# Memory projections of a fused two-layer network: the dot products of keys move from VectorE and GpSimd to TensorE

## The reference, cut to what matters

```python
k = k / jnp.maximum(jnp.linalg.norm(k, axis=-1, keepdims=True), 1e-12)
alpha = jax.nn.sigmoid(alpha_raw) * 0.5
...
def t_step(M, kv):
    k_t, v_t = kv
    Mk = jnp.einsum('bhde,bhe->bhd', M, k_t)
    forget = Mk[..., :, None] * k_t[..., None, :]
    write = v_t[..., :, None] * k_t[..., None, :]
    return (M - alpha * forget + beta * write, None)
```

## Time and profile before

| | |
|---|---|
| timed runs | 4588.27, 4594.0, 4600.99 us; median 4594.0 |
| profiled execution | 4591.41 us, span 4589.7 us, mean granted clock of PE 0.891 |
| busy over the span | PE 3650.9, DVE 2555.3, POOL 1683.4, ACT 1439.0 us |
| the stage `mproj` | from 2539.8 us (its first DMA issue) to 2970.5 us (the first of the next stage) |

### The profile page before, as it was taken

How to read it: one execution, slowest core, us unless ns; L and a number is a source line. 1 busy time by engine, 2 the same in 40 slices (tenths; PEclk the granted TensorE clock), 3 DMA queues, 4 the chain that set the end, 5 groups by cost and what they waited for, 6 DMA issues and landing times. The chain is left out here.

```text
span 4589.7 us, 53885 instructions
## 1 busy us (share of the span) xinstructions
PE 3650.9 (80%) x17474; PEld 1655.7 (36%) x17563; DVE 2555.3 (56%) x3976; ACT 1439.0 (31%) x2018; POOL 1683.4 (37%) x1362
## 2 busy tenths in 40 slices
PE   8899999979997899977695404077897956999994
PEld 3322222223332433325353202033455433555553
DVE  5589999945552255534425597855794693111113
ACT  2247777743332233322132202011452311111111
POOL 0032222226664066652362273533561332222221
PEclk9979999989998999988797756588897978999997
DMA  5542322211103511013326202033452103333333
GB/s 174 185 72 63 68 71 61 56 55 37 37 24 100 180 35 37 26 61 99 101 86 197 102 18 73 18 87 91 134 163 97 46 19 107 103 94 95 98 86 82
DMA packets 323883, 382.97 MB, mean 83 GB/s; under 512 B 52016, under 2 KB 252992, under 8 KB 322688
## 3 DMA queue, kind: packets, MB, share of 16 engines
q1 hardware_dynamic: 270912, 285.83, 20.2%
q0 software_dynamic: 35776, 73.97, 6.4%
q10 hardware_dynamic: 17024, 20.97, 1.3%
HBM read 240.69 MB, written 135.76 MB: 82 GB/s over the span
## 5 line engine op out<-in xcount | busy, mean ns | idle before, releaser
L571 DVE TENSOR_REDUCE modulated_mx<-modulated_ring 128x1 f32<-128x512 f32 x1024 | 651.5, 682 | 51.7 <-PE modulated_ring L478 45.7
L555 ACT ACTIVATE modulated_probs<-modulated_scores 128x1024 f32<-128x1024 f32 x512 | 496.1, 1021 | 181.5 <-PE modulated_scores L499 181.4
L2862 DVE TENSOR_TENSOR expert_h<-expert_gelu,expert_bank 128x512 f32<-128x512 f32 x128 | 88.0, 688 | 391.8 <-PE expert_bank L2830 391.8
L2790 POOL DMA_INDIRECT scratch_acc<-expert_y,expert_idx x64 | 101.0, 1579 | 485.2 <-DVE expert_y L2867 443.2
L508 PE MATMUL modulated_acc<-modulated_probs,modulated_v 128*32 128x512 f32 x2048 | 273.6, 606 | 0.6 <-ACT modulated_probs L555 0.6
L478 PE MATMUL modulated_ring<-modulated_k,modulated_q 64*128 64x512 bf16 x1024 | 239.6, 399 | 34.1 <-DMA modulated_v<-scratch_v 23.0
L499 PE MATMUL modulated_scores<-modulated_q,modulated_k 128*128 128x512 bf16 x945 | 255.6, 383 | 10.1 <-issue 5.4
L910 POOL TENSOR_TENSOR causal_total<-causal_total,causal_probs 128x1024 f32<-128x1024 f32 x96 | 225.7, 2351 | 86.5 <-ACT causal_probs L831 85.5
L910 POOL TENSOR_TENSOR meta_total<-meta_total,meta_probs 128x1024 f32<-128x1024 f32 x96 | 225.7, 2351 | 86.5 <-ACT meta_probs L831 85.5
L2830 PE MATMUL expert_bank<-expert_xT,expert_wg 128*128 128x512 f32 x512 | 243.2, 598 | 7.8 <-ACT expert_xT L2842 7.8
L853 DVE TENSOR_REDUCE meta_mx<-meta_maxima 128x2 f32<-128x1024 f32 x120 | 146.0, 1216 | 184.0 <-PE meta_maxima L737 184.0
(11 more groups left out here) (471 smaller groups left out, 7028.7 us busy)
## 6 DMA issues: line engine op xcount, KB each, us to landing
expert_wg<-x_WgT SPq DMA_DIRECT2D x16, 1024.0 KB, 4.9
expert_wu<-x_WuT SPq DMA_DIRECT2D x16, 1024.0 KB, 6.9
expert_wd<-x_WdT SPq DMA_DIRECT2D x16, 1024.0 KB, 5.4
modulated_k<-scratch_k_part SPq DMA_DIRECT2D x192, 64.0 KB, 3.0
modulated_q<-scratch_q_part SPq DMA_DIRECT2D x192, 64.0 KB, 3.1
scratch_v<-proj_v SPq DMA_DIRECT2D x8, 1024.0 KB, 6.6
modulated_v<-scratch_v SPq DMA_DIRECT2D x16, 512.0 KB, 4.5
scratch_M<-steps_snap SPq DMA_DIRECT2D x16, 512.0 KB, 3.3
```

The costliest lines, as they stand in the source:

```text
L555: nc.scalar.activation(probs[u % NPROBS][i][:], sc[i][:], ACT.Exp, scale=SCALE).then_inc(s_exp, 1)
L571: V.tensor_reduce(mx[h % 2][:, x // 2, 1 - j % 2, j // 2, x % 2:x % 2 + 1], ring[bank_of["max", 4 * m + j]][:], AX.X, ALU.max).then_inc(s_ ...
L2790: added[j].done(G.indirect_dma_start(out=scr["acc"], out_offset=bass.IndirectOffsetOnAxis(ap=idx[j][a][:], axis=0), in_=y[j][:, a, :], in_ ...
```

## The change: what it does

- **Dot products on PE.** POOL makes from the transposed keys `laid` two masked copies per tile of 128 tokens (`masked`, L1820): one keeps the even heads, one the odd heads, both multiplied by -alpha (`share_of`). PE multiplies them with `laid` (L1856 of the changed file), 16 matmuls of 128 columns per tile, each on a row group of 32 rows, which is one pair of heads; neighbouring matmuls take different row groups p and write different banks. This gives for every head the 128 x 128 dot products of the tile's tokens, with -alpha in them.
- **Eviction.** ACT (in group 0 ACT and DVE, two banks each; in group 1 ACT all four) copies the banks to `dots`, two buffers.
- **Transfers lay them by piece.** Of each 128 x 128 square only the eight 16 x 16 blocks on the diagonal are wanted. SP issues 8 DMAs per tile (L1793), one per piece: 16 partitions x 16 heads x 16 tokens into one partition of `A`, which is 256 runs of 64 bytes, 16 KB. With 16 tiles that is 128 DMAs per group, 256 in all. The products, sums, the clearing and the scaling of `A` on DVE and POOL go.
- **DVE alone substitutes,** both halves of the heads in whole, in place in `k` (the copy S goes).
- **Groups overlap.** There is no hardware loop: the code is written out (class `Order` numbers the steps), `xT`, `k`, `A` have two buffers, both `xT` loads are issued at the start, by SP. While DVE substitutes group 0 it also makes the keys of group 1 (after each of its first five steps), and PE, POOL, ACT and SP make group 1's dot products. The projections of v and q of both groups come last on PE and ACT, beside the substitution of group 1.

The diff, cut to its core:

```diff
-            with sp.Fori(0, N // GROUP) as g:
-...
-                dve_s.wait(dve, g, ("k", TT - 1, QUADS - 1))
-...
-                    pool_s.wait(dve, g, ("far", n))
-                    dve_s.done(total(other[n % 2], f[1], f[0]), ("far", n))
-...
+        jobs = []
+        for g in range(G):
+            for c in range(QUADS):
+                jobs += [("k", g, c)] + [("kT", g, c - 1, m) for m in range(HH)] * (c > 0)
+            jobs += [("kT", g, QUADS - 1, m) for m in range(HH)]
+            jobs += [("dots", g, t) for t in range(TILES)]
+        for g in range(G):
+            for c in range(QUADS):
+                jobs += [("v", g, c)] + [("q", g, c, m) for m in range(KD)]
+...
+        ACT_BANKS = {0: (0, 1), 1: (0, 1, 2, 3)}
+        STEPS = range(SUB - 1, 0, -1)
+...
+            for g in range(G):
+                act_s.wait(sp, ("kT", g, QUADS - 1, HH - 1))
+                sp.dma_start(rows(scr["kT"])[:, :, g * GROUP:(g + 1) * GROUP], laid[:]).then_inc(s_kT, 16)
+                for t in range(TILES):
+                    act_s.wait(sp, ("dots", g, t, ACT_BANKS[g][-1]))
+                    if g == 0:
+                        dve_s.wait(sp, ("dots", g, t, 3))
+                    for s in range(PIECES):
+                        r = slice(s * SUB, (s + 1) * SUB)
+                        n = t * PIECES + s
+                        sp.dma_start(A[g][n:n + 1, :, :, :], dots[t % 2][r, :, r]).then_inc(s_laid[t % 2], 16)
+            dve_s.wait(sp, ("rows", 0, 1, 1))
+            sp.dma_start(by_piece(scr["s4"][0:GROUP, :]), k[0][:]).then_inc(s_s, 16)
+...
+            for g in range(G):
+                act_s.wait(pool, ("kT", g, QUADS - 1, HH - 1))
+                for t in range(TILES):
+                    if t >= 2:
+                        mm.wait(pool, ("dots", g, t - 2))
+                    here = laid[:, :, t * P:(t + 1) * P].unsqueeze(2).broadcast_to([P, HH, 2, P])
+                    pool_s.done(nc.gpsimd.tensor_tensor(masked[t % 2][:], here, share_of[:].unsqueeze(3).broadcast_to([P, HH, 2, P]), ALU.mult),
+                                ("masked", g, t))
+...
+                if kind == "dots":
+                    pool_s.wait(pe, ("masked", g, c))
+                    for half in range(HH):
+                        for odd in range(2):
+                            for p in range(4):
+                                r = slice(p * PAIR, (p + 1) * PAIR)
+                                last = nc.tensor.matmul(at[p][:, (2 * half + odd) * P:(2 * half + odd + 1) * P], masked[c % 2][r, half, odd, :],
+                                                        laid[r, half, c * P:(c + 1) * P], start=True, stop=True)
+...
+                for t in range(TILES):
+                    mm.wait(act, ("dots", g, t))
+                    use = g * (TILES // 2) + t // 2
+                    if use > 0:
+                        act.wait_ge(s_laid[t % 2], 16 * PIECES * use)
+                    for p in ACT_BANKS[g]:
+                        from_ = bank[banks_of(("dots", g, t))[p]]
+                        act_s.done(copy(dots[t % 2][:].rearrange("p (a b o) n -> p a b o n", a=HH, o=2)[:, :, p, :, :], from_[:].rearrange("p (a o n) -> p a o n", a=HH, o=2)),
+                                   ("dots", g, t, p))
+...
+                    for part in range(HALVES):
+                        if i + 1 < SUB:
+                            dve_s.wait(dve, ("rows", g, i + 1, part))
+                        elif g > 0:
+                            dve_s.wait(dve, ("rows", g - 1, 1, part))
+                        dve_s.done(tt(laid_out(part), A[g][:, i, part * HP:(part + 1) * HP, 0:i].rearrange("p h r -> p r h").unsqueeze(3).broadcast_to([P, i, HP, HD16]),
+                                      k[g][:, i:i + 1, heads(part)].rearrange("p r (h e) -> p r h e", e=HD16).broadcast_to([P, i, HP, HD16]), ALU.mult),
+                                   ("share", g, i, part))
+                    for part in range(HALVES):
+                        dve_s.wait(dve, ("share", g, i, part))
+                        dve_s.done(tt(k[g][:, 0:i, heads(part)], k[g][:, 0:i, heads(part)], own[part][:, 0:i * HP * HD16].rearrange("p (r n) -> p r n", r=i), ALU.add),
+                                   ("rows", g, i, part))
+                    if g == 0 and n <= QUADS:
+                        if n > 0:
+                            make_keys(1, n - 1)
+                        if n < QUADS:
+                            measure(1, n)
```

More of the change, by code:

```diff
@@ L1652, in every_16th, with __init__, done, wait @@
     return a.rearrange("p (s x) -> p x s", x=SUB)
+class Order:
+    def __init__(self, sem, names, passed):
+        self.sem, self.passed, self.at = sem, passed, 0
+        self.value = {x: n + 1 for n, x in enumerate(names)}
+        assert len(self.value) == len(names)
+    def done(self, ins, name):
+        self.at += 1
+        assert self.value[name] == self.at, (name, self.at)
+        return ins.then_inc(self.sem, 1)
+    def wait(self, eng, name, alone=False):
+        eng.wait_ge(self.sem, self.value[name])
+        if alone:
+            apart(eng, self.passed)
@@ L1672, in memory_projections @@
         length2, length, bounded, inv = (st.sb(n, [P, TT * H16]) for n in ("length2", "length", "bounded", "inv"))
[L1673 to L1676 removed]
         laid = st.sb("laid", [P, HH, GROUP])
+        masked = two("masked", [P, HH, 2, P])
+        dots = two("dots", [P, H16, P])
@@ L1700, in memory_projections @@
-        for n, (f, e) in enumerate(zip(far, near)):
-            dve_names += [("near", n)] * (e is not None) + [("far", n)] + [("near_sum", n)] * (e is not None)
-        dve_names += [("scaled", hp) for hp in range(HH)]
-        for i in range(SUB - 1, 0, -1):
-            dve_names += [(x, i, part) for x in ("share", "rows") for part in range(2)]
-        act_s, dve_s = st.steps("act", act_names), st.steps("dve", dve_names)
-        pool_s = st.steps("pool", [("far", n) for n in range(len(far))] + [(x, i) for i in range(SUB - 1, 0, -1) for x in ("share", "rows")])
@@ L1708, in memory_projections @@
-        PARTS = ((0, 0, HP), (1, 0, HP // 2), (1, HP // 2, HP))
-        loaded = st.moves("loaded", credit=0, kept=True)
-        stored = {x: st.moves("stored_" + x, HH if x in ("v", "s") else 1) for x in ("q", "v", "kT", "s")}
-        s_w, s_made, s_alpha = st.sem("weights"), st.sem("made"), st.sem("alpha")
+            dve_names += lengths(0, c) + keys(0, c)
+        dve_names += [("dots", 0, t, p) for t in range(TILES) for p in range(4) if p not in ACT_BANKS[0]]
+        for g in range(G):
+            for n, i in enumerate(STEPS):
+                dve_names += [(x, g, i, part) for x in ("share", "rows") for part in range(HALVES)]
+                if g == 0 and n <= QUADS:
+                    dve_names += keys(1, n - 1) if n > 0 else []
+                    dve_names += lengths(1, n) if n < QUADS else []
@@ new lines, in memory_projections @@
+        order = lambda n, names: Order(st.sem(n), names, scr["passed"])
+        mm, act_s, dve_s = order("mm", jobs), order("act", act_names), order("dve", dve_names)
+        pool_s = order("pool", [("masked", g, t) for g in range(G) for t in range(TILES)])
+        s_w, s_made, s_share = st.sem("weights"), st.sem("made"), st.sem("share")
+        s_x = [st.sem(f"x_loaded{g}") for g in range(G)]
+        s_k, s_kT, s_v, s_s = (st.sem("stored_" + x) for x in ("k", "kT", "v", "s"))
+        s_q = [st.sem(f"stored_q{j}") for j in range(2)]
@@ L1761, in _ @@
+            dve_s.wait(sp, ("rows", 1, 1, 1))
+            sp.dma_start(by_piece(scr["s4"][GROUP:2 * GROUP, :]), k[1][:]).then_inc(s_s, 16)
+            sp.wait_ge(s_kT, 16 * G)
+            sp.wait_ge(s_v, 16 * G)
+            sp.wait_ge(s_s, 16 * G)
+            for j in range(2):
+                sp.wait_ge(s_q[j], 16 * G * QUADS // 2)
         @block.gpsimd
@@ new lines, in _, with turned_keys @@
+            nc.scalar.activation(raw[:], raw[:], ACT.Sigmoid).then_inc(s_share, 1)
+            copy = lambda out, src: nc.scalar.activation(out, src, ACT.Copy)
+            def turned_keys(g, c):
+                for m in range(HH):
+                    mm.wait(act, ("kT", g, c, m))
+                    if g == 1 and (c, m) == (0, 0):
+                        act.wait_ge(s_kT, 16)
+                    to = every_16th(laid[:, m, :])[:, c * TT:(c + 1) * TT, :]
+                    act_s.done(copy(to, bank[banks_of(("kT", g, c, m))[0]][:].rearrange("p (x s) -> p x s", s=P)), ("kT", g, c, m))
```

333 lines of the change are left out of this document (156 added, 177 removed).

## The result

The changed kernel took 4652.0 us (median of 4 runs, 4641.5 to 4654.0) against 4596.8 for the kernel before on the same chip: a ratio of 1.0116, 95% interval 1.0100 to 1.0133. It is slower by 55 us; I had forecast 4488 and a range up to 4560. In the profiled execution the stage's first DMA issue comes 2.6 us later than before and the next stage's first load 57 us later. The stage has become 54.5 us longer (485.2 us in place of 430.7), so the loss lies in it whole.

A forecast was written before the change was run, and what follows sets the result against it. Each group was taken as a chain PE, DVE, DVE with nothing of the next group beside it. The summed steps moved the stage's end from 2970.5 to 2865, so 4594 - 105.5 = 4488 us, range 4465 to 4560.

The forecast's parts named there:

- keys of group 0: Stage start: without q and v, hand-overs bound at 5.5 us a quad; 31 us, keys laid at 2582.
- dot products of group 0: Group 0's products and transfers into `A`: 16 tiles at 3.85 us plus start and landing, 72.6 us together.
- to group 1's last keys: Group 0's substitution with group 1's keys made beside it: `laid` of group 1 complete 54 us after its start.
- dot products of group 1: Group 1's products and transfers: ACT empties all banks, two tiles take 8.2 us; 77.9 us, DVE waits some 49.
- So SP sets the pace: Dot products: SP's issue, 3.76 us a tile, is slowest of the line; the transfers themselves need 0.16 us each.
- SP's period: Time between SP's issues of transfers into `A`: taken as 0.47 us, bounds 0.42 and 0.68.
- rival 1: Dot products: SP issues slower, 0.65 us apart, +23 in group 0 and +19 in group 1; 4530 us; chance 15%.
- Rival 3: Transfers into `A`: packets to one partition queue singly, 2.4 us per DMA; 4976 us, loss from 0.88; chance 8%.
- Rival 2: Transfers into `A`: one partition takes bytes at one engine's rate, 0.60 us per 16 KB; 4514 us; chance 8%.
- Rival 4: Dot products: PE's row groups bring nothing, 7.8 us a tile at half clock, 4.2 at full; 4552 us; chance 6%.
- Rival 5: Group 0's substitution: DVE waits at a key of group 1, costing 10 to 20 us; 4503; 5% with similar small ones.
- The sign I had named: Transfers into `A`: forecast wrong if the period is over 0.7 us or landing grows from tile to tile.

The follow-up runs named there:

- e1_spread: Changed kernel with each transfer laying its 16 rows into 16 partitions of `A` in place of one; 4519.1 us, ratio to before 0.9853.
- e2_runs1k: Changed kernel with each transfer read as 16 runs of 1 KB (other products), still into one partition; 4513.3 us, ratio to before 0.9841.
- e12_alternate: Changed kernel with a tile's eight transfers issued in the order 0, 4, 1, 5, 2, 6, 3, 7; 4546.6 us, ratio to before 0.9905.
- e4_three: Changed kernel with three buffers of `dots` in turn in place of two; 4604.8 us, ratio to before 1.0036.
- e9_own_products: Changed kernel with dot products back on DVE and POOL, v and q after each group's keys; 4497.6 us, ratio to before 0.9802.
- e6_long: Changed kernel with heads innermost in `dots` and `A`, so 16 runs of 1 KB per transfer; 4510.9 us, ratio to before 0.9824.
- e10_half_runs: Changed kernel with runs of 32 bytes in place of 64, as many writes; 4636.6 us, ratio to before 1.0103.

## Why the prediction was wrong

Step by step, in the prediction's order:

| Step | forecast | measured |
|---|---|---|
| PE starts | 2551 | 2553.3; the stage's first issue was 2.6 us later than before |
| keys of group 0 | 31 | 28.6 |
| dot products of group 0 | 72.6 | 155.0 |
| to group 1's last keys | 54 | 52.1 |
| dot products of group 1 | 77.9 | 163.5 |
| substitution of group 1 | 68.2 | 68.2 |
| store and hand-over | 9.5 | 6.8 |
| next stage's first load | 2865 | 3027.5 |

**The step that failed** is the sentence "So SP sets the pace" in the dot products: the transfer itself was put at 0.16 us and so hidden under SP's 0.47. The row that I rested it on the earlier trace rows has the right runs and bytes and a different destination, 128 partitions; I wrote that down and still took its landing. What the runs showed in its place: transfers into one group of four partitions, and the group 32 further, are served at one write per 3.7 ns, 0.96 us for a transfer, and the eight pieces of a tile lie in two such groups, used one after the other. With the pause that two buffers add, two tiles took 18.0 us in group 0 and 19.8 in group 1, where I had 7.7 and 8.2. The stage was to take 325 us (2539.8 to 2865) and took 485; of these 160 us, 128 are this (`e1_spread` takes them away).

**A second term was mis-sized:** SP's period is 0.65 us, not 0.47. That is rival 1, near its price of 42 us: the stages of `e1_spread` and `e2_runs1k`, where SP sets the pace, are 32 and 24 us over the forecast's 325. I had chosen the period of small DMAs, backed by the issue of one load from DRAM, over the 0.68 of the longest kind. Why such a transfer takes 0.61 to issue is open; the number of runs is not the reason.

**The rivals.** Rival 3 named the place and the way, and its turning point of 0.88 us fits the runs: at 0.74 us a transfer (`e12_alternate`) the stage is 52 us shorter than before, at 0.96 (`e4_three`) 15 us longer. Its price of 2.4 was more than twice too high, since it took the 9.4 ns that an engine needs for a packet as what the destination needs; that is 3.7. My reason against it, that the wait would have to be five times the packet's share, was no reason, for it was six times (3.7 ns against 9.4 / 16 = 0.6). Rival 2 (0.60 us, 27 GB/s) is neither shown nor excluded: SP's 0.63 to 0.65 lies above its price, and with 64-byte runs the price is 0.96, by the number of writes and not by bytes. Rival 4 was wrong: 32 records in 2.09 us at half clock is a quarter of 7.8. Rival 5 was wrong: 52.1 us.

**What was right:** the keys' pace (4.9 us a quad, forecast 5.5), POOL's mask at 1.04 in group 0 (in group 1, beside DVE's substitution, the mean was 1.76), ACT's two banks in 1.08 us, the overlap, and DVE's price per element. v and q hid behind the last substitution, but at a clock of 0.83 and not over 0.9. With another destination and all else the same, the change pays, though less than summed: the stage of `e1_spread` is 73 us shorter than before, where I had 105.5. `e9_own_products`, without the products on PE, saves 94.

**The sign I had named** (landing that grows from tile to tile, a period over 0.7) is what the trace shows. From 2607 us on, the median landing of three tiles in turn is 4.8, 8.6 and 9.4 us and then stays there, since with two buffers no more than 16 transfers can be waiting; the 16 transfers of a round take 18.0 us. I had it as a check for afterwards, when it should have widened the range: the cost was unknown between 0.16 and 2.4 us, the loss began at 0.88, and I gave that side 8%. The range should have reached past 4600.

## What to carry to other kernels

The price of these transfers was set at the end where their runs are written, so a row with the same bytes and runs prices a transfer only if the partitions match too. Where many small pieces go into single partitions, make the run long (1 KB and not 64 bytes: 132 us of the stage here, by `e6_long`) or, if nothing else can be changed, issue them so that neighbours don't follow each other (106 us for one reordered loop, `e12_alternate`). And when a sum rests on a cost that no row bounds, work out the value at which the sign turns first, and let the chances follow from where it lies between the bounds.

## What the runs showed of the hardware

- Runs of 64 bytes written into a group of four neighbouring partitions, with the four 32 further, go at one per 3.7 ns, 0.96 us for 256 of them (`e4_three`), and runs of 32 bytes take about as long (`e10_half_runs`). Two groups work side by side (`e12_alternate`, 0.74 us a transfer).
- Transfers of the same short runs within SBUF land after 1.9 us when each is laid over 16 partitions, no later than those of 1 KB runs into one (2.1), and after 9.9 us when each goes into one.
- DVE's operations of the substitution stretch while POOL makes masks. The pair of 1152 elements took 4.30 us while POOL was busy for 4.97 of 6.0 us (from 2795), and 2.61 with POOL idle (timeline of DVE after the change, group 0 and group 1):

```profile
2796.42 4.30 DVE L1972 TENSOR_TENSOR mproj_k<-mproj_k,mproj_own 128x1152 f32<-128x1152 f32 x2
```

```profile
2996.69 2.61 DVE L1972 TENSOR_TENSOR mproj_k<-mproj_k,mproj_own 128x1152 f32<-128x1152 f32 x2
```
